# Local attention on one core: the negated maximum as the bias of eight exponentials instead of two matmuls

## What is computed

```
sim = jnp.einsum('bhwid,bhwjd->bhwij', bq, bk)
mask = (i < j) | (i > j + WINDOW) | (j == -1)
sim = jnp.where(mask, -jnp.finfo(sim.dtype).max, sim)
attn = jax.nn.softmax(sim, axis=-1)
out = jnp.einsum('bhwij,bhwjd->bhwid', attn, bv)
```

## Time and profile before

| | us |
|---|---|
| median of 3 runs | 458.41 (458.27, 458.41, 460.68) |
| the profiled execution | 460.31 |
| its span, first to last instruction | 458.5 |
| TensorE busy | 382.0 (83%) |
| VectorE busy | 356.7 (78%) |
| ScalarE busy | 235.5 (51%) |
| GpSimd busy | 21.0 (5%) |
| maximum `lneg` on VectorE, each of 16 | 1.216 |
| matmul of the shift on TensorE, each of 32 | 0.38 to 0.63 |
| exponential on ScalarE, each of 16 | 1.019 |

### The profile page before, as it was taken

One profiled execution on the slowest core, in us unless ns is written; L12 is line 12 of the kernel. 1 busy time (PEld: TensorE's weight loads), 2 busy tenths in 40 slices (PEclk: granted clock), 3 DMA queues, 4 the chain that ended last, 5 costly groups with the idle time before them and its releaser, 6 DMA issues.

```text
span 458.5 us, 10020 instructions
## 1 busy us (share of the span) xinstructions
PE 382.0 (83%) x4101; PEld 280.6 (61%) x4101; DVE 356.7 (78%) x721; ACT 235.5 (51%) x432; POOL 21.0 (5%) x30
## 2 busy tenths in 40 slices
PE   3898899998453689988777998999999899997966
PEld 1597788876312235554455676867767676776854
DVE  5999998997798679775877779878796978774542
ACT  1744444442454157765443455747656565754541
POOL 2000020000020110000000000000000001010110
PEclk9999999999755579997888999999999999997997
DMA  8500000000000000000000000000000000000000
GB/s 338 249 5 3 20 21 4 3 4 1 0 0 2 0 0 1 2 1 0 1 1 1 0 1 1 2 1 0 1 0 2 1 1 1 1 0 2 24 1 23
DMA packets 1773, 8.29 MB, mean 18 GB/s; under 512 B 192, under 2 KB 448, under 8 KB 1472
## 3 DMA queue, kind: packets, MB, share of 16 engines
q1 hardware_dynamic: 1728, 7.65, 4.2%
HBM read 7.12 MB, written 0.52 MB: 17 GB/s over the span
## 4 chain that ended last, share of the span: by engine, by line
PE 51%; DVE 33%; ACT 10%; issue 5%; DMA 1%; DVEq 0%; ACTq 0%
PE ps L251 12%; PE ps L549 9%; DVE blk L825 5%; PE ps L649 5%; PE ps L616 3%; PE ps L661 3%; PE ps L491 2%; PE ps L478 2%; PE ps L607 2%; DVE blk L1114 2%; DVE blk L1105 2%; PE ps L597 2%; DVE ss L1115 2%; ACT blk L1361 2%; ACT PT L1444 2%
## 5 line engine op out<-in xcount | busy, mean ns | idle before, releaser
L549 PE MATMUL ps<-w_f,full 128*128 128x512 f32 x96 | 45.8, 614 | 0.7 <-DVE blk L1109 0.7
L1293 ACT ACTIVATE St<-ps 128x512 bf16<-128x512 f32 x32 | 19.1, 597 | 44.9 <-PE ps L251 44.9
L1105 DVE TENSOR_TENSOR blk<-ps,tabs 128x1024 f32<-128x1024 f32 x16 | 19.6, 1224 | 28.9 <-ACT blk L1361 28.9
L1361 ACT ACTIVATE blk<-ps 128x1024 f32<-128x1024 f32 x16 | 16.4, 1027 | 30.5 <-PE ps L549 30.5
L616 PEld LDWEIGHTS ps<-blk,PT 128*128 128x128 f32 x256 | 30.3, 192 | 1.6
L616 PE MATMUL ps<-blk,PT 128*128 128x65 f32 x256 | 31.3, 275 | 0.0
L549 PEld LDWEIGHTS ps<-w_f,full 128*128 128x128 f32 x96 | 18.5, 200 | 18.8 <-issue 17.7
L251 PEld LDWEIGHTS ps<-blk,st 128*128 128x128 bf16 x768 | 26.7, 98 | 3.8
L251 PE MATMUL ps<-blk,rel 128*128 128x64 bf16 x768 | 27.6, 193 | 0.0
L251 PE MATMUL ps<-blk,st 128*128 128x64 bf16 x768 | 27.6, 193 | 0.0
L607 PE MATMUL ps<-const,PT 128*128 128x128 f32 x128 | 17.9, 285 | 9.3 <-ACT blk L1384 9.3
(11 more groups left out here) (231 smaller groups left out, 886.4 us busy)
## 6 DMA issues: line engine op xcount, KB each, us to landing
w_f<-f_dram SPq DMA_DIRECT2D x2, 1689.0 KB, 13.2
w_x<-l_dram SPq DMA_DIRECT2D x1, 774.0 KB, 5.9
w_f<-ffn_dram SPq DMA_DIRECT2D x1, 561.0 KB, 7.9
X<-x_dram SPq DMA_DIRECT2D x1, 512.0 KB, 3.5
ctxT<-ctxT_dram SPq DMA_DIRECT2D x1, 512.0 KB, 4.4
OT<-maskT_dram SPq DMA_DIRECT2D x1, 512.0 KB, 7.0
rest<-l_dram SPq DMA_DIRECT2D x1, 385.0 KB, 5.0
const<-const_dram SPq DMA_DIRECT2D x1, 324.0 KB, 6.2
```

The costliest lines, as they stand in the source:

```text
L549: m = mm(ps[:, c, :], hT[:, n, :], w_f[:, l, F_QKV + 512 * c:F_QKV + 512 * (c + 1)], start=True, stop=True)
L1105: step(v.tensor_tensor(heads(R[:, i % 2, :]), u, tab[:, 0].to_broadcast([P, 2, LH, LD]), ALU.mult))
L1361: a(SQ, ps[:, 0:2, :].rearrange("p b c -> p (b c)"), ACT.Square).then_inc(sem("squared"), 1)
```

## The change

`shift` is taken out, and the exponential adds the negated maximum itself: a bias of an activation is one number a partition, and the maximum is one number a partition and head, so the one activation becomes eight, of 128 columns each. `lneg` is kept in float32. `lexp` is counted twice a tile, after four heads each, and every wait on it is renumbered; `turn_p` waits for the first count before the first four transposes and for the second before the others. VectorE's `largest(i)`, which waited for the shift of tile i - 2 before it wrote the same buffer of `lneg`, waits for the exponentials of that tile.

```diff
-        lneg = sb("lneg", [2, LH], BF16)
+        lneg = sb("lneg", [2, LH])
...
             def turn_next_z(i, q):
...
-                pe.wait_ge(sem("lexp"), i + 1)
+                pe.wait_ge(sem("lexp"), 2 * i + 2)
...
             def score(i):
                 pe.wait_ge(sem("kT"), i + 1)
                 if i >= 1:
-                    pe.wait_ge(sem("lexp"), i)
+                    pe.wait_ge(sem("lexp"), 2 * i)
...
-            def shift(i):
-                pe.wait_ge(sem("lmax"), i + 1)
-                for c in range(2):
-                    m = add(ps[:, 3 + c, :], ident_b[:, :],
-                            lneg[:, i % 2, 4 * c:4 * c + 4].rearrange("p (h o) -> p h o", o=1).to_broadcast([P, 4, P]))
-                m.then_inc(sem("lshifted"), 1)
...
             def turn_p(i):
-                pe.wait_ge(sem("lexp"), i + 1)
                 if i + 1 < 2 * NB:
                     pe.wait_ge(sem("kT"), i + 2)
                 for c in range(2):
+                    pe.wait_ge(sem("lexp"), 2 * i + c + 1)
...
             for i in range(2 * NB):
-                shift(i)
                 if i == 1:
                     turn_z(1)
...
             def largest(i):
                 dve.wait_ge(sem("lscores"), i + 1)
                 if i >= 2:
-                    dve.wait_ge(sem("lshifted"), i - 1)
+                    dve.wait_ge(sem("lexp"), 2 * (i - 1))
...
             def exponential(i):
-                act.wait_ge(sem("lshifted"), i + 1)
+                act.wait_ge(sem("lmax"), i + 1)
                 if i >= 2:
                     act.wait_ge(sem("pT_ps"), 2 * (i - 1))
-                a(S1[:, i % 2, :], ps[:, 3:5, :].rearrange("p b k -> p (b k)"), ACT.Exp).then_inc(sem("lexp"), 1)
+                for c in range(2):
+                    for j in range(4):
+                        k = 4 * c + j
+                        e = a(S1[:, i % 2, P * k:P * (k + 1)], ps[:, 3 + c, P * j:P * (j + 1)], ACT.Exp,
+                              bias=lneg[:, i % 2, k:k + 1])
+                    e.then_inc(sem("lexp"), 1)
```

More of the change, by code:

```diff
@@ L624, in shift_tokens @@
                 pe.wait_ge(sem("z"), 2 * q + 2)
-                pe.wait_ge(sem("lexp"), min(i + 1, 2 * NB))
+                pe.wait_ge(sem("lexp"), 2 * min(i + 1, 2 * NB))
                 if i >= 2 * NB:
```

## The result

The changed kernel took 451.87 us (median of 4 runs, 450.75 to 452.87), the kernel before 458.54 beside it (4 runs, 458.27 to 460.68): a ratio of 0.985 with an interval of 0.982 to 0.988, 6.7 us off. Forecast were 450.6 and 7.8 off. A second set of runs of the same file gave 450.81 (5 runs, 450.71 to 452.21), 0.984 [0.982, 0.987]. The profiled execution took 450.75 with a span of 449.0; before, 460.31 and 458.5. Those two spans lie 9.5 apart, which is more than the medians do.

What follows compares the result with a forecast made beforehand. Bound: the local stage's chain of waits, with QKV queued behind shift matmuls that wait for VectorE's maximum. Terms 0.2 + 1.8 + 0.9 + 4.5 + 0 + 0.4 = 7.8 us off 458.4 gave 450.6; range 447.5 to 455.0.

Steps and rivals of the forecast that it cites:

- tile 0: Start of the local stage: QKV moves up by 0.4, but ScalarE had idled only 0.25, so 0.2 us gained.
- tile 1: Without the shift Z is turned and QKV ends earlier; the square then follows ScalarE's other work: 1.8 us gained.
- tiles 2 and 3: Shift of 0.58 leaves each chain; unit norm caps tile 2 at 0.35, tile 3 gains all: 0.9 us together.
- five pairs: Tile pairs 4-5 to 12-13: 0.46 from the even and 0.43 from the odd tile each, 4.5 us in all.
- tile 15: Last local tile: the shift before the second product goes, 0.4 us gained; the exponentials' second half just fits.
- The exponentials: ScalarE's eight of 128 columns with bias take 2.2 us together, bounds 1.6 and 2.9, replacing one of 1.02.
- The even tile: Tile 12: QKV starts when the weighing ends; VectorE's unit norm then limits the gain to 0.46 of 0.9 us.
- The odd tile: Tile 13: TensorE reaches QKV 0.43 us earlier, gained in full; exponentials stay hidden with 1.4 us to spare.
- (a): Rival: even tiles gain nothing because copies of turned Q and K are held; 5.5 us gained, 452.9; chance 0.21.
- (b): Rival: ScalarE becomes the bound, exponentials taking 3.6 us; total gain near 1.7, 456.7, no difference; chance 0.07.
- Part 4: The forecast's section on the start, tiles 0 to 3; in tile 1 the eight exponentials cost one for one.
- (c): Rival: TensorE's clock falls to 1.2 GHz once in each pair, 2.2 us slower, 460.6; chance 0.06.

Runs made afterwards that it cites:

- the second execution: The changed kernel run again unaltered, with a second trace: 450.81 us (5 runs).
- the matmuls alone: The changed kernel plus two matmuls of the shift's size ahead of each QKV in tiles 2 to 15, without the wait: 453.48 us.
- the wait alone: The changed kernel plus a TensorE wait for VectorE's maximum at each tile's head, without the matmuls: 454.94 us.
- the kernel that has both and the eight: The kernel before, shift kept, with its one exponential cut into eight of 128 columns without bias: 458.95 us.
- The runs with fillers: Nine unread matmuls put into tile 1's wait, in the kernel before (456.56 us) and in the changed kernel with the wait alone (450.83 us).

## Why the prediction was right, point by point

**The time.** 450.6 forecast, 451.9 measured, within the range. In the profiled executions the terms sum to 6.5 where the forecast had 7.8; the medians give 6.7.

| term | forecast | measured |
|---|---|---|
| tile 0 | 0.2 | -0.14 (1.01 in the second execution) |
| tile 1 | 1.8 | 1.86 |
| tiles 2 and 3 | 0.9 | 0.84 |
| five pairs | 4.5 | 4.29 |
| tile 14 | 0 | 0.13 (-0.31) |
| tile 15 | 0.4 | -0.48 |

**The exponentials** took 2.17 against 2.2 forecast. One is 381 ns where the GELU's rows gave 367, and they overlap by (8 x 0.381 - 2.17) / 7 = 0.125 where I had taken 0.10, so the two errors nearly cancel, which is luck. By the Trainium skill, "ScalarE: Activation LUTs", section What ACT_TABLE_LOAD costs, the estimate had been 2.45: its length for one, 387, agrees, and its overlap of 93 ns is smaller than the trace shows. The trace decides.

**The even tile** came out as worked out. The maximum ends at 380.40 (E); QKV starts at E - 0.41 (forecast E - 0.26), turn_qk at E + 2.65 as VectorE's unit norm ends (forecast E + 2.58), turn_p at E + 4.92 (forecast E + 4.95; before E + 5.41). The cap by the unit norm was the step that mattered, and it held. **The odd tile** too: the exponentials end at 395.80, 1.56 ahead of the square (forecast 1.4). A pair gives 0.86 against 0.9, of it 0.49 up to turn_p of the even tile (forecast 0.46) and 0.37 in the rest (forecast 0.43).

What I'd not have guessed is how the 0.86 divides: the matmuls alone 0.43, the wait alone 0.07, and 0.36 that is there only with both. The eight exponentials don't enter: the kernel that has both and the eight takes the same 26.17. The prediction said that the wait in front of QKV matters more than the matmuls' own time. As a statement on either one alone that was wrong; it is the two in line behind the maximum that push QKV past the unit norm.

**Tile 1** has the right size, 1.86 for 1.8, by a partly wrong account. I had named the half clock but counted the gain as one of order. The runs with fillers show the shares: with shift and wait left in place and the clock held, tile 1 falls from 12.61 to 11.19. So 1.42 of it is clock, and order and work make the other 0.44. And the 1.8 was met partly by luck: it was read from one execution of before. In the kernel with the shift and eight exponentials the same TensorE queue took 14.03 over tile 1; against that execution the same change would have given 3.28. **Tiles 2 and 3** were split the wrong way round, 0.59 and 0.25 for 0.35 and 0.58; their sum is right.

**Tile 0** was 0.14 longer in one execution and 1.01 shorter in the other. In the first, QKV took 3.37 at a fallen clock. The term of 0.2 drowns in that.

**Tile 15 is the step that failed.** The prediction gave it 0.4 and said that the exponentials' second half "just fits". From the last maximum's start to turn_p it took 7.33 before and 7.81 after, 0.48 longer; in the second execution of after it was 7.81 again. Its rows:

```profile
420.71 2.15 ACT L1385 ACTIVATE PT<-ps,lneg 128x128 f32<-128x128 f32 x8
...
423.01 0.46 PE L621 MATMUL ps<-zv,const 128*128 128x128 f32 x2 [1.21 <-ACT PT L1385]
423.75 1.04 PE L600 MATMUL ps<-const,PT 128*128 128x128 f32 x8
```

Ahead of turn_p stand the token turns (line 621), which write the bank that the exponentials read, and so wait for all eight: 1.21 idle. I had looked at who needs the exponentials' result and not at who needs their banks. With two exponentials of 1.25 the wait is 0.30. turn_p then starts 6.94 after the maximum's start, 0.39 earlier than before, which is the forecast's 0.4. So the term was wrong by what the eight exponentials cost through their banks, 0.87 of 0.88. That is most of the 1.1 between the forecast gain and that of the medians (1.3 in the profiled executions).

**The surplus between the profiled spans.** Of 9.5 us, 6.98 lie in the stage, 0.88 ahead of tile 0, where nothing was changed, and 1.64 behind tile 15's maximum although turn_p comes later there. The tail's feed-forward products, after, before, and after again:

```profile
438.17 1.60 PE L654 MATMUL ps<-w_f,PT 128*128 128x128 f32 x12 [2.29 <-DVE PT L1147]
440.65 2.86 PE L642 MATMUL ps<-YT,w_f 128*128 128x256 f32 x12 [0.65 <-ACT YT L1411]
```

```profile
444.80 2.62 PE L661 MATMUL ps<-w_f,PT 128*128 128x128 f32 x12 [2.93 <-DVE PT L1155]
448.50 4.57 PE L649 MATMUL ps<-YT,w_f 128*128 128x256 f32 x12 [0.66 <-ACT YT L1414]
```

```profile
436.29 2.69 PE L654 MATMUL ps<-w_f,PT 128*128 128x128 f32 x12 [2.94 <-DVE PT L1147]
440.06 4.50 PE L642 MATMUL ps<-YT,w_f 128*128 128x256 f32 x12 [0.66 <-ACT YT L1411]
```

The same instructions of the same file took 4.46 in one execution and 7.19 in the other. The granted clock over these two groups was 1.00 in the first and 0.59 in the other, and 0.59 in before. The difference in the tail is the execution's clock and not the change; two traces alone would have credited it with 9.5 us.

**The rivals.** (a) fell: turn_p is at E + 4.92, not 5.4. (b) fell: in tiles 4 to 13 no square waits for an exponential, and the eight without bias changed nothing in a pair. It holds for tile 15, where the exponentials do end last, though in front of a matmul and not of the square, and for tile 1, as Part 4 had it: there the square starts at 250.18 without a gap behind ScalarE's other work, 1.44 after QKV is over (245.99 + 2.75), and two exponentials in place of eight make the tile 0.87 shorter. (c) fell as a forecast: the clock is 1.00 over the pair, and 0.76 over tile 14 as it had been 0.77. TensorE's longest idle time in a pair is 0.56. Its mechanism is real all the same, and worked on the side of the change in tile 1: taking the wait for the maximum away left QKV at 2.75 there, where kernels with the wait took 3.36 to 5.26. The Trainium skill, "TensorE: Matmul & The Clock Gate", Part 1, names activity as what lifts the throttle; the runs with fillers agree (QKV 2.74 against 5.26).

## What to carry to other kernels

On an engine that runs in order, look at what stands behind a waiting instruction and doesn't need the wait, then take off the next thing that is late: that gave the pairs within 0.1 us. When a step grows or moves, list two kinds of waiters, those for its result and those for the buffer it reads; the miss in tile 15 was of the second kind. A wait that leaves TensorE idle for 2 us can cost again in what follows it, so compare parts of the program that repeat between executions, and try filling such a wait with matmuls that nobody reads.

## What the runs showed of the hardware

The same six matmuls of QKV in tile 1 took 2.74 to 2.75, 3.36, 4.78 and 5.26 us, and behind idle times of nearly equal length (2.29, 2.28 and 2.35) they took 3.36, 4.78 and 5.26: what such a wait costs varies by some 2 us with where the clock falls. The spread between runs goes with it. Before with nine fillers had runs at 454.1 to 454.5 with a mean granted clock of 0.94, and at 458.6 to 459.8 with 0.925 to 0.929.

Fourteen filler matmuls (3.19 us of work that nobody reads) made tile 14 0.88 us shorter, in a kernel whose busiest engine is TensorE, at 83%: the turns behind them ran at a clock of 1.00.

On ScalarE an exponential of 128 columns with a per-partition bias took 381 ns and one without 304, so 77 more, and eight in a row 2.17 against 1.47.
